# Attention pass: LayerNorm 2's rows are normalised by VectorE in every batch, GpSimd keeps only the scalars

## The reference, cut to what matters

```python
x = _layernorm(x + _L0_attn_ref(x), axis=-1)                      # autocorrelation attention
x = _layernorm(x + _L0_xattn_ref(ctx_4096, ctx_4096, x), axis=-1) # LayerNorm 2 is this one
x = _layernorm(x + _L0_ffn_ref(x, ...), axis=-1)                  # dense layer and a LoRA mixture
```

## Time and profile before

| | before |
|---|---|
| median of 3 runs | 1972.63 us (1972.58 to 1975.0) |
| the profiled execution's own time | 1972.2 us |
| its span, from first to last instruction | 1970.4 us |
| TensorE, VectorE, ScalarE, GpSimd busy | 91%, 70%, 37%, 14% of the span |
| mean granted TensorE clock | 0.967 |
| the normalisations on GpSimd (line 320) | 30, from 78.6 to 561.5 us |
| the normalisations on VectorE (line 586) | 2, at 572.7 and 575.5 us |
| first add and last add into x2buf (line 499) | 65.7 and 570.8 us |

### The profile page before, as it was taken

One profiled execution on the slowest core, in us unless ns is written; L12 is line 12 of the kernel. 1 busy time (PEld: TensorE's weight loads), 2 busy tenths in 40 slices (PEclk: granted clock), 3 DMA queues, 4 the chain that ended last, 5 costly groups with the idle time before them and its releaser, 6 DMA issues. The chain is left out here.

```text
span 1970.4 us, 27045 instructions
## 1 busy us (share of the span) xinstructions
PE 1783.9 (91%) x10194; PEld 956.6 (49%) x10210; DVE 1373.9 (70%) x2605; ACT 734.3 (37%) x909; POOL 268.2 (14%) x418
## 2 busy tenths in 40 slices
PE   3989998999953969999999999998899999999996
PEld 2656675767630425444554445443344444444443
DVE  3888888888859856677765677789655555565463
ACT  5766777676635221222222212133221222213111
POOL 1244343434310000000000000000010010010000
PEclk8999999999985989999999999999899999999998
DMA  8899999999848499999999999945989889988882
GB/s 278 193 278 266 281 250 289 253 278 250 250 181 233 124 239 251 265 256 232 254 254 258 251 236 225 233 165 160 288 253 256 276 219 259 269 245 247 255 238 107
DMA packets 565564, 472.71 MB, mean 240 GB/s; under 512 B 498416, under 2 KB 502512, under 8 KB 544624
## 3 DMA queue, kind: packets, MB, share of 16 engines
q1 hardware_dynamic: 565424, 470.87, 87.5%
HBM read 237.51 MB, written 109.58 MB: 176 GB/s over the span
## 5 line engine op out<-in xcount | busy, mean ns | idle before, releaser
L1562 PE MATMUL bank_f<-w_hi_f,a_cols_f 128*128 128x512 f16 x3584 | 1093.6, 382 | 76.7 <-DMA a_cols_f<-rows_f 58.1
L1562 PE MATMUL bank_f<-w_lo_f,a_cols_f 128*128 128x512 f16 x1792 | 685.4, 382 | 0.0
L1562 PEld LDWEIGHTS bank_f<-w_hi_f,a_cols_f 128*128 128x128 f16 x3584 | 353.0, 98 | 508.5 <-DMA a_cols_f<-rows_f 41.7
L1562 PEld LDWEIGHTS bank_f<-w_lo_f,a_cols_f 128*128 128x128 f16 x1792 | 176.4, 98 | 204.8 <-issue 4.4
L1152 ACT ACTIVATE rows_f<-xn_f 128x1024 f16<-128x1024 f32 x78 | 82.4, 1057 | 499.5 <-DMA xn_f<-x_scratch 336.0
L1327 DVE SCALAR_TENSOR_TENSOR y_f<-bank_f,w_iscale_f,y_f 128x512 f32<-128x512 f32 x192 | 134.5, 742 | 169.8 <-PE bank_f L1562 169.2
L653 PE MATMUL ps_s_fast<-k_both_fast,q_hi_fast 128*128 128x256 f16 x1024 | 171.2, 275 | 7.3 <-DMA k_both_fast<-v_lo_fast 6.3
L1327 DVE SCALAR_TENSOR_TENSOR y_f<-bank_f,w_iscale,y_f 128x512 f32<-128x512 f32 x192 | 134.8, 743 | 37.8 <-PE bank_f L1562 30.2
L1288 DVE TENSOR_TENSOR rows_f<-xn_f,rows_f 128x1024 f16<-128x1024 f32 x78 | 94.4, 1210 | 92.7 <-ACT rows_f L1152 92.6
L1288 DVE TENSOR_TENSOR rows_f<-sums_f,rows_f 128x1024 f16<-128x1024 f32 x63 | 76.9, 1220 | 115.4 <-ACT rows_f L1152 115.4
L653 PE MATMUL ps_s_fast<-k_both_fast,q_lo_fast 128*128 128x256 f16 x512 | 140.7, 275 | 0.0
(11 more groups left out here) (211 smaller groups left out, 2377.3 us busy)
## 6 DMA issues: line engine op xcount, KB each, us to landing
xbuf_fast<-x SPq DMA_DIRECT2D x32, 1024.0 KB, 7.3
x_scratch<-x2buf_fast SPq DMA_DIRECT2D x32, 1024.0 KB, 8.0
y_f<-x_scratch SPq DMA_DIRECT2D x32, 1024.0 KB, 7.9
xn_f<-x_scratch SPq DMA_DIRECT2D x62, 512.0 KB, 4.8
kept_scratch<-a_cols_f SPq DMA_DIRECT2D x45, 512.0 KB, 3.4
xn<-x_scratch SPq DMA_DIRECT2D x45, 512.0 KB, 6.5
a_cols_f<-kept_scratch SPq DMA_DIRECT2D x45, 512.0 KB, 8.8
cbuf<-ctx_in SPq DMA_DIRECT2D x16, 1024.0 KB, 5.9
```

The source lines that it names most:

```text
L1562: ins = nc.tensor.matmul(bank[i][:], a_cols[:, i, part + kk, :], ww[:, W_SLOT[i], kk, :], start=(kk == 0 and part == 0 and ww is w_hi), st ...
```

## The change

GpSimd's `normalise2` and its filler go; GpSimd makes the scalars only. VectorE gets a `normalise2` with the same arithmetic, used in all batches: for row tile 1 of batch n-1 it stands at j = 4 of the loop, after that step's add and `x2_mean(0)`; for row tile 0 of batch n it stands after `x2_mean(1)`, ahead of `x_stats(0)`. In the last batch the two stay at the end of the slot.

```diff
@@ GpSimd
-                def normalise2(n, parity, r):
-                    pool.wait_ge(ln2_ready, R * n + r + 1)
-                    settle(1)
-                    g.tensor_scalar(x2buf[parity][:, r], x2buf[parity][:, r], rs2[:, r:r + 1], nb2[:, r:r + 1], ALU.mult,
-                                    ALU.add).then_inc(x2_ready, 1)
                     if is_batch(n - 1, nb):
                         norm2(n - 1, 1 - parity, 1)
-                        normalise2(n - 1, 1 - parity, 1)
                     if cur and n < nb - 1:
                         norm2(n, parity, 0)
-                        normalise2(n, parity, 0)
@@ VectorE
+                    def normalise2(n, parity, r):
+                        dve.wait_ge(ln2_ready, R * n + r + 1)
+                        v.tensor_scalar(x2buf[parity][:, r], x2buf[parity][:, r], rs2[:, r:r + 1], nb2[:, r:r + 1], ALU.mult,
+                                        ALU.add).then_inc(x2_ready, 1)
                         if j == 3:
                             guard_lags(1)
+                        if j == 4 and is_batch(n - 1, nb):
+                            normalise2(n - 1, other, 1)
                     if cur:
                         x2_mean(1)
+                    if cur and n < nb - 1:
+                        normalise2(n, parity, 0)
-                    if isinstance(n, int) and n == nb - 1:
+                    if n == nb - 1:
                         for r in range(R):
-                            dve.wait_ge(ln2_ready, R * n + r + 1)
-                            v.tensor_scalar(x2buf[parity][:, r], x2buf[parity][:, r], rs2[:, r:r + 1], nb2[:, r:r + 1], ALU.mult,
-                                            ALU.add).then_inc(x2_ready, 1)
+                            normalise2(n, parity, r)
```

More of the change, by code:

```diff
@@ L152, in attention_pass @@
         mean_sq = sb("mean_sq", [P, R], F32)
-        pool_pad = [sb(f"pool_pad{i}", [P, R], F32) for i in range(2)]
         w_tile = consts["xn0"]
@@ L292, in _ @@
                 chain = Chain(nc, pool, pool_step, consts["pad"])
-                def settle(i):
-                    g.tensor_tensor(pool_pad[i][:], columns[:, MINUS_ONE], columns[:, MINUS_ONE], ALU.mult)
                 def norm_steps(n, at):
```

## The result

| | before | after |
|---|---|---|
| median | 1972.61 us (1971.74 to 1975.0, 4 runs) | 2021.71 us (2020.08 to 2022.27, 4 runs) |
| ratio, 95% interval | 1 | 1.0248 [1.0235, 1.0261] |
| the profiled execution's own time and span | 1972.2, 1970.4 us | 2022.27, 2020.5 us |
| GpSimd busy | 14% | 10% |

The kernel became 49 us slower, 2.5%; 2020 was forecast.

What follows compares the result with a forecast made beforehand. A circle through VectorE's v_lo, the cbuf load, ScalarE's square and the j=4 add sets the slot; 6 x 2.7 + 7 x 4.5 + 1.35 + 4.5 - 1.2 - 5 = 47.3 us on 1972.2, said as 2020, range 1996 to 2038.

Steps and rivals of the forecast that it cites:

- The circle: Attention slots: v_lo on VectorE, transpose and cbuf load, ScalarE's square, j=4 add and VectorE's row of work set the slot.
- the lock: VectorE and GpSimd share a port pair, locked per instruction; GpSimd's normalisation stretches g_lags to 1.78 us in odd slots.
- The prediction's sign for the lock: After the change, a j=4 add less than 2.27 us after the square's start would show that the lock mattered.
- Even slots, +2.7 each: Even slots 2 to 12: x lands late behind the held store, so bn_stats starts 2.7 us later (1.5 to 3.4).
- Odd slots, +4.5 each: Odd slots 1 to 13: x waits behind store and weights, so bn_stats starts 4.5 us later (3.3 to 5.2).
- The two normalisations: On VectorE, 1.347 us each: at j=4 hidden to 0.1 us; after x2_mean(1) in full unless VectorE would wait there.
- Given back, 5 us: Longer slots leave the DMA queue emptier for transposes: 0.4 us in each of 13 slots, 5 us (0 to 8).
- the lock and the clock, 1.2: Credit for unlocked g_lags steps, reaching further only in slot 9 through TensorE's rest and clock: 1.2 us (0 to 1.7).
- The end of the pass, +4.5: Slot 15: late store holds SP's three prefetches, so the feed-forward part starts 4.5 us later (at least 1.0).
- Only VectorE's work counts: Rival, chance 0.14: a load doesn't wait for the store in front, only VectorE's added work costs; 1985 us.
- Faster: the lock was the price: Rival, chance 0.04: g_lags steps set odd slots, 10.7 us comes back, new instructions lie in idle time; 1961.5 us.
- The clock: Rival, chance 0.13: VectorE's late fold makes TensorE rest and lowers its clock in ten slots or so; 12 us more, 2032.

Runs made afterwards that it cites:

- run 9: The kernel before, with only the next context loads issued ahead of the v_lo transposes on SP; 1972.93 us, 0.9999 of before.
- run 7: The changed kernel with row tile 0 normalised on GpSimd again and x of row tile 0 issued ahead of the second store; 1979.34 us, 1.0024 of before.
- run 2: The changed kernel with only row tile 1 normalised by VectorE, at j=4, and row tile 0 on GpSimd; 2024.53 us, 1.0264 of before.
- run 1: The changed kernel with the weights and x of row tile 0 issued ahead of the second store on SP; 1984.41 us, 1.0062 of before.
- run 5: The kernel before, with GpSimd normalising only 8 of row tile 1's 2048 columns and the rest left out; 1973.2 us, 0.9995 of before.
- run 6: The changed kernel with the weights issued behind both loads of x instead of ahead of them; 2014.35 us, 1.0203 of before.

## Why the prediction was right

**The circle.** It held in most slots: 2.27 us from the square to the j = 4 add in 9 of slots 1 to 13 before and in 11 after, and 6.27 from that add to the end of the j = 7 add. But the prediction looked at slots 7 to 9 only and saw the lock reach past j = 4 in slot 9 alone. Before, the add came 2.42, 3.51, 2.79 and 2.34 us behind the square in slots 5, 9, 11 and 13, all odd. In slot 11:

```profile
434.14 1.79 DVE L481 SCALAR_TENSOR_TENSOR g_lags<-gmax_fast,ps_g_fast,x_var_fast 128x1 f32<-128x1 f32 x1
...
437.91 1.06 ACT L369 ACTIVATE junk_fast<-cbuf_fast 128x1024 bf16<-128x1024 f32 x1 [2.68 <-DMA cbuf_fast<-ctx_in]
...
440.71 0.74 DVE L499 SCALAR_TENSOR_TENSOR x2buf_fast<-ps_c_fast,iscale_fast,xbuf_fast 128x512 f32<-128x512 f32 x1
```

In slots 5, 11 and 13 the j = 4 add came 9.63 us after the j = 0 add, as in the locked slots of run 9. So there the locked step was already the last to end, by 0.07 to 0.52 us. The prediction's sign for the lock, an add less than 2.27 us behind the square after the change, could not show this: no slot of either kernel has less, and where the locked step ends last it is more. The excess of the four slots is 2.0 us in all, 1.2 of them in slot 9, against the rival's 10.7. Run 9 shows the limit of the circle. When the context tile comes early enough, the locked step sets the slot instead.

**Even slots, +2.7 each:** +2.78. The store goes out 2.29 us behind the j = 4 add (2.3 forecast), and x lands 7.59 us after the store's issue in slot 8 (7.5 forecast).

**Odd slots, +4.5 each:** +4.95, inside the bounds and 3 us short in seven slots. x landed 11.3 us after the store in slot 9, where the sum had 10.0. The weights landed 8.4 us after their own issue and x 10.5 after its: the 2.5 us that I put down for one tile more was the price at 423 GB/s; from slot 8 to slot 9 it was 3.7.

**The two normalisations.** That of j = 4 is hidden (run 7: 0.88 us before bn_stats, as before), and the second lies inside the wait for x (run 2: 17.2 us more waiting without it). The direct sign for j = 4 is the 6.27 us above, the same with and without the instruction. So VectorE's 30 added instructions have no direct part in the 49 us beyond slot 0 and the end of the pass.

**Given back, 5 us, and the lock and the clock, 1.2:** together 7.8 us. The j = 4 adds came 9.3 us sooner in all, counted from the first add of their slot, and 1.0 of that went in slot 3. From the end of v_lo of row tile 1 to the landed context tile it took 10.07 us before, averaged over slots 1 to 13, and 9.42 after: 0.65 a slot, where 0.4 was forecast, 8.5 in all, just over the 0 to 8. The v_lo transpose took 1.9 us to issue on average instead of 3.0. The g_lags steps are 0.23 us everywhere. What the lock and the clock gave back by themselves no run shows apart.

**The end of the pass, +4.5:** +5.2. The last prefetch, issued at 614.53, landed 10.2 us later, at 624.7: 49.0 us later than the 575.7 of before. SP now waits for it, where before it had landed 1.5 us ahead of the end of SP's last issue:

```profile
SPq L286 <- DMA cbuf<-w_chunks: 3.1, 1, 3.1
```

The last store of batch 15 also lands 5.3 us later, counted from slot 15's first add (581.43 before, 630.12 after), so it could have been what the feed-forward part waited for. But VectorE's first instruction there doesn't wait for that store and came 4.8 us later too. The feed-forward part starts 48.6 us later, and nothing else changed in it beyond 1.5 us.

**The rivals.** "Only VectorE's work counts", 1985, is what run 1 measured once x was out of the store's shadow: 1984.41. So the time came out and the condition was wrong: in this queue a load does count what stands in front. That the time came out is luck in part: in run 1's profiled execution the end of the pass cost 4.7 us where this rival had 1.0, and the j = 4 adds came 4.7 us sooner in all where it had 1.2. The Trainium skill, "DMA: Bandwidth & Descriptors", section "Queues, rings and completion order", lets transfers of a queue complete out of order; in slot 8 the store landed 4.8 us after 365.54, at 370.4, and x 7.2 after 365.91, at 373.1, so it gave no help here.

"Faster: the lock was the price" fell in run 5 as the price of the kernel before, and came true as a mechanism in run 9.

"The clock" had its cause but not its effect. TensorE did wait for the fold, 36.1 us in 13 slots, and its clock fell behind such a rest, here in slot 7:

```profile
340.00:345.00 5.00, 1.07 (x10) 0.71 (x8) 4.92 (x10) 0.50 (x1) 3.19 (x4) 1.00 1.21 172
345.00:350.00 5.00, 4.92 (x31) 3.75 (x32) 4.85 (x13) 4.91 (x10) 2.06 (x5) 0.66 1.05 192
```

But the context product that comes up to 1 us late is needed only behind the context tile: the j = 4 add still follows that tile's landing by some 2.3 us in 11 of 13 slots. Only slot 3 shows a longer loop (7.29 us from the j = 4 add to the end of j = 7), and there TensorE had rested for 2.14 us.

**The sum.** Against the forecast's 47.3 us the slots took 3.5 more (52.6 for 49.05), the end of the pass 0.7 more and the feed-forward part 1.5 that was not forecast; 1.6 more came back, and the first add came 1.4 earlier. That makes 50.0, and the span grew by 50.1. So the time came out closer than some terms, because misses of both signs met in it; that part is luck.

## What to carry to other kernels

Before moving a producer to another engine, follow its consumer's DMA to the queue that issues it: everything behind it in that order is delayed with it, and the price is paid by whoever waits for the last of these. Take away a limit only after looking for the second one of the same length; here the lock and the context tile hid each other: without one of them nothing was gained, without both 12 us. Look at a wait in every slot before calling it the limit: the equal 2.27 us of slots 7 and 8 hid four slots in which the locked step ended last. Work put into an engine's gap is free itself, but when its result comes is not.

## What the runs showed of the hardware

A v_hi transpose held SP's queue for 7.44 us where weights and x were still moving (slot 9 of after), and for 4.53 us behind x alone (slot 8). Two took 9.04 us in run 6, while a v_lo transpose on an emptier queue was issued in 1.85 us:

```profile
407.13 7.44 SPq L229 DMA_TRANSPOSE k_both_fast<-v_hi_fast  x1
```

The same normalisation of 128x2048 took 1.34 us on VectorE and 2.05 on GpSimd. TensorE at rest for 2 us in one piece was followed by a granted clock of 0.63 and then 0.52 (run 5), that is, by its lower level of 1.2 GHz for most of the next 4 us. Such a rest is not a sure sign: before the change, seven odd slots had rests of 2.12 to 2.15 us, and only that of slot 9 was followed by a lower clock; in run 5 rests of 2.16, 2.21, 2.35 and 2.77 us were, and one of 2.23 us was not.
